# Turning xn and half of the probabilities on TensorE instead of through DRAM, in an attention block on one core

## What is computed

```python
def attn(x, Wq, Wk, Wv, Wo):
    q, k, v = x @ Wq, x @ Wk, x @ Wv
    scores = where(causal_mask, -max, einsum('bsd,btd->bst', q, k))
    attn = softmax(scores * dim_k ** (-0.5), axis=-1)
    return einsum('bst,btv->bsv', attn, v) @ Wo
...
x = x + layernorm(attn(layernorm(x), Wq, Wk, Wv, Wo))
x = x + layernorm(layernorm(x) @ W[idx] + b[idx])     # idx = argmax(log_softmax(logits) + gumbel(u))
```

## Time and profile before

| | before |
|---|---|
| median of 3 runs | 430.8 us (430.01 to 431.18) |
| the profiled execution | 428.95 us |
| its span from first to last instruction | 427.1 us |
| TensorE, VectorE, ScalarE, GpSimd busy | 384.1, 330.9, 259.3, 216.0 us |
| mean granted TensorE clock | 0.975 |
| moved by DMA | 67.75 MB, 54.5% of the queues' time on queue 1 |

### The profile page before, as it was taken

How to read it: one execution, slowest core, us unless ns; L and a number is a source line. 1 busy time by engine, 2 the same in 40 slices (tenths; PEclk the granted TensorE clock), 3 DMA queues, 4 the chain that set the end, 5 groups by cost and what they waited for, 6 DMA issues and landing times.

```text
span 427.1 us, 7846 instructions
## 1 busy us (share of the span) xinstructions
PE 384.1 (90%) x2652; PEld 359.5 (84%) x2652; DVE 330.9 (77%) x844; ACT 259.3 (61%) x642; POOL 216.0 (51%) x367
## 2 busy tenths in 40 slices
PE   7996967999869998999879998799979998999994
PEld 6775856999769996899769997699968997899994
DVE  4488755799847987789867998579868998667876
ACT  5866555576546665575655765567665757555642
POOL 5115264554645554645855446455656448535234
PEclk9998998999989998999999999899999999999998
DMA  6323884249843498328872498435982388331012
GB/s 196 119 55 122 240 221 115 69 171 254 229 130 103 193 240 238 115 69 271 232 190 81 163 262 243 126 114 199 272 219 82 120 241 237 105 107 51 25 51 74
DMA packets 45611, 67.75 MB, mean 159 GB/s; under 512 B 8196, under 2 KB 38276, under 8 KB 44676
## 3 DMA queue, kind: packets, MB, share of 16 engines
q1 hardware_dynamic: 45300, 66.99, 54.5%
q10 hardware_dynamic: 272, 0.26, 0.2%
HBM read 34.34 MB, written 32.90 MB: 157 GB/s over the span
## 4 chain that ended last, share of the span: by engine, by line
PE 45%; DMA 26%; issue 9%; DVE 7%; ACT 4%; POOL 3%; POOLq 3%; SPq 3%; DVEq 0%
PE bank L1003 25%; PE score L1003 17%; DMA p_kept<-p_turn 16%; DMA p_turn<-p_kept 9%; ACT pT_hi L704 3%; SPq L443 3%; PE bank L1157 2%; POOLq L517 2%; DVE p_turn L911 2%; POOL pT_lo L546 1%; DMA x_kept<-x_turn 1%; DVE neg_scores L901 1%; DVE g_lo L767 1%; ACT g_hi L582 1%; PE bank L1128 1%
## 5 line engine op out<-in xcount | busy, mean ns | idle before, releaser
L546 POOL TENSOR_TENSOR pT_lo<-p_turn,pT_hi 128x128 fp32r<-128x128 f32 (+7 forms) x60 | 82.2, 1393 | 22.2 <-ACT pT_hi L704 22.1
L1003 PE MATMUL bank<-v_hi,pT_lo 128*128 128x258 f32 x288 | 82.6, 287 | 7.0 <-DVEq L865 3.9
L1003 PE MATMUL bank<-v_lo,pT_hi 128*128 128x258 f32 x288 | 81.6, 283 | 0.0
L1003 PE MATMUL bank<-v_hi,pT_hi 128*128 128x258 f32 x288 | 81.2, 282 | 0.0
L1003 PE MATMUL score<-xT_hi,g_lo 128*128 128x384 f32 (+4 forms) x176 | 65.0, 369 | 15.0 <-DVE neg_max L901 14.9
L503 POOL TENSOR_TENSOR o_rstd<-o_ss,minus_half 128x1 f32<-128x1 f32 x64 | 37.9, 594 | 77.4 <-ACT squares_junk L738 77.4
L695 ACT ACTIVATE probs<-neg_scores,neg_max 128x128 f32<-128x128 f32 (+3 forms) x64 | 49.2, 776 | 42.0 <-DVE neg_max L901 41.9
L1003 PE MATMUL score<-xT_hi,g_hi 128*128 128x384 f32 (+4 forms) x176 | 63.2, 359 | 0.0
L1003 PE MATMUL score<-xT_lo,g_hi 128*128 128x384 f32 (+4 forms) x176 | 63.2, 359 | 0.0
L1003 PEld LDWEIGHTS bank<-v_hi,pT_lo 128*128 128x128 f32 x288 | 54.7, 190 | 8.5 <-issue 6.9
L1003 PEld LDWEIGHTS bank<-v_lo,pT_hi 128*128 128x128 f32 x288 | 54.9, 191 | 0.6
(11 more groups left out here) (115 smaller groups left out, 1031.3 us busy)
## 6 DMA issues: line engine op xcount, KB each, us to landing
x_sb<-in_L_attn_x_dram SPq DMA_DIRECT2D x32, 256.0 KB, 5.4
out_dram<-f_sb SPq DMA_DIRECT2D x31, 256.0 KB, 5.6
x_kept<-x_turn SPq DMA_DIRECT2D x7, 1024.0 KB, 4.3
x_turn<-x_kept SPq DMA_DIRECT2D x28, 256.0 KB, 7.1
p_kept<-p_turn SPq DMA_DIRECT2D x7, 960.0 KB, 9.8
p_turn<-p_kept SPq DMA_DIRECT2D x28, 240.0 KB, 4.2
p_kept<-p_turn SPq DMA_DIRECT2D x7, 704.0 KB, 3.1
p_turn<-p_kept SPq DMA_DIRECT2D x28, 176.0 KB, 4.4
```

The source lines that it names most:

```text
L546: nc.gpsimd.tensor_tensor(p_half(pT_lo, n), p_quads(n), p_half(pT_hi, n).bitcast(f32), ALU.subtract).then_inc(p_lo_ready, 1)
L1003: last = nc.tensor.matmul(dst, l, r, start=(i == 0), stop=(i == len(passes) - 1))
```

## The change

- xn is transposed by TensorE: 16 transposes of 128x128 a batch, in four jobs X0 to X3, into banks of the ring; ScalarE and VectorE split them from there. The blocks on VectorE (B), the write and the reads (W, R), `x_turn` and `x_kept` are gone.
- The probabilities of row tiles 0 to 3 are transposed by TensorE too (T0 to T3, ten transposes a batch, four jobs), in every batch, and split by ScalarE and VectorE. Tiles 4 to 7 still go through DRAM, in the last batch through TensorE as before.
- The ring has 32 jobs a batch instead of 24. `pT` has four places instead of three, counted over all batches, with a wait of ScalarE (`slot_read`) where the old content may still be read.
- All order strings are new. X2, X3 of the next batch are at the end of a step, their G2 and G3 in the next step.

```diff
-    PS = 3
+    PS = 4
-    PE_ORDER = """S0 S1 S2 S3 O6' O7' S4 Y1' V0 S5 Y2' F0' O0 S6 S7 O1 F1' V1 V2 Y3' F2' O2 V3 F3' O3 O4 O5 G0 G1 G2 Y0 G3"""
-    ACT_ORDER = """Y0' G3' E0 E1 E2 E3 O6' H0 O7' H1 P0 P1 Y1' E4 V0 H2 Y2' E5 O0 P2 F0' P3 H3 E6 O1 E7 V1 F1' V2 Y3' O2 P4
-        P5 V3 F2' O3 F3' X0 X1 O4 X2 X3 O5 G0 G1 P6 P7 G2"""
-    DVE_ORDER = """G2' M0 M1 G3' Q0 Q1 M2 Y0' M3 L0 L1 K0 K1 Q2 Q3 L2 K2 B0 R6' R7' M4 B1 Y1' Q4 V0 B2 M5 L3 F0' K3 Q5 Y2'
-        M6 N3' B3 Z0' M7 R0 R1 F1' Q6 V1 V2 Q7 Y3' F2' Z1' N0 R2 V3 F3' Z2' R3 N1 X0 X1 X2 X3 R4 R5 Z3'
-        G0 N2 G1"""
-    POOL_ORDER = """P7' L0 L1 C6' L2 C7' P0 P1 C0 L3 U0' P2 P3 N3' C1 U1' C2 P4 P5 U2' C3 N0 U3' N1 C4 C5 N2 P6"""
-    SP_ORDER = """P0 Q0 P1 A3' Q1 P2 W0 Z0' Q2 A0 R0 P3 Z1' Q3 A1 Z2' A2 Z3'"""
+    PE_ORDER = """S0 S1 F1' S2 Y2' G2' T0 S3 G3' O6' T1 T2 S4 O7' V0 S5 V1 T3 O0 S6 O1 Y3' F2' S7 Y0 O2 O3 V2 V3 F3' X0 X1
+        F0 O4 G0 Y1 G1 O5 X2 X3"""
+    ACT_ORDER = """X3' E0 P6' P7' E1 F1' Y2' G2' T0 E2 G3' H0 O6' T1 T2 E3 H1 E4 H2 O7' V0 V1 E5 T3 O0 O1 Y3' E6 F2' Y0 O2
+        E7 O3 V2 V3 P4 P5 X0 X1 H3 F3' F0 O4 G0 Y1 G1 O5 X2"""
+    DVE_ORDER = """M0 R5' X2' X3' M1 F1' M2 N2' L0 Y2' G2' T0 M3 L1 K0 G3' Z1' K1 L2 K2 T1 M4 T2 R6' Q4 R7' V0 N3' M5 V1 Q5
+        T3 M6 R0 L3 R1 Y3' F2' Q6 N0 M7 Y0 Z2' R2 Q7 R3 V2 K3 N1 V3 F3' X0 X1 F0 Z3' R4 G0 Y1 Z0 G1"""
+    POOL_ORDER = """P6' P7' N2' U1' L0 L1 L2 C6' C7' N3' C0 C1 U2' N0 C2 C3 L3 P4 P5 N1 U3' C4 U0 C5"""
+    SP_ORDER = """A2' Z1' A3' P2 A0 Q2 Z2' P3 A1 Q3 Z3' Z0"""
-    PE_LAST = """S0 V0 S1 S2 O6' S3 O7' Y1' S4 Y2' F0' O0 S5 Y3' S6 F1' V1 O1 V2 O2 V3 O3 F2' F3' T4 Y0 S7 Y1 T5 O4 T6 F0
-        O5 T7 O6 F1 Y2 O7 Y3 F2 F3 Y4 F4"""
+    PE_LAST = """S0 S1 S2 S3 T0 G2' T1 O6' G3' F1' Y2' T2 O7' V0 S4 F2' V1 O0 O1 V2 S5 T3 T4 O2 S6 S7 Y3' V3 Y0 O3 T5 F3'
+        Y1 T6 O4 O5 T7 F0 O6 Y2 O7 Y3 F1 F2 F3 Y4 F4"""
...
-                    elif kind == "W":
-
-                        sp.wait_ge(x_turned, b.count(NP, 0))
-                        sp.dma_start(x_kept.rearrange("p q r -> p (q r)"), x_turn[:, :]).then_inc(x_written, 16)
-                    elif kind == "R":
-                        sp.wait_ge(x_written, b.count(16, 0))
-                        fetch(x_turn[:, :], x_kept.rearrange("(i a) q r -> q a i r", i=QUADS), x_raw_loaded)
...
+            def slot_read(b, n, kind):
+
+                free, at = (b, n - PS) if n >= PS else (b.other(-1), n + NT - PS)
+                if not free.exists() or follows(in_act, (kind, n, b.known), ("O", at, free.known)):
+                    return
+                if kind == "T" and follows(in_pe, ("T", n, b.known), ("O", at, free.known)):
+                    return
+                used = Job(free, "O", at)
+                act.wait_ge(bank_full[used.bank], used.used + 1)
...
                     elif kind == "T":
+                        slot_read(b, n, "T")
                         for g, (u0, u1) in enumerate(t_groups(n)):
                             job = Job(b, "T", n, g)
-                            round_hi(job, pT_hi[:, n % PS, u0 * PART:u1 * PART], cols(job.bank, (u1 - u0) * PART))
+                            round_bank(job, pT_hi[:, (b.known * NT + n) % PS, u0 * PART:u1 * PART], cols(job.bank, (u1 - u0) * PART),
+                                       t_hi_ready)
...
-                        c, k = n // KC, n % KC
-                        if n == 0:
-                            act.wait_ge(x_raw_loaded, b.count(QUADS * 16, 0))
-                            act.wait_ge(scores_ready, b.count(NT, 0))
...
-                        nc.scalar.activation(split_block(xT_hi, c, k), raw_block(c, k),
-                                             ACT.Identity).then_inc(x_hi_ready, 1)
+                        x_hi(Job(b, "X", n), n, x_hi_ready)
...
-            def x_transposes(job, p):
-
-                pe.wait_ge(xn_ready, p + 1)
+            def x_transposes(b, job, p):
+
+                pe.wait_ge(xn_ready, b.count(NP, p + 1))
...
-                        if n % 2 == 0:
-                            pe.wait_ge(x_lo_ready[c], b.count(KC, 0))
-                        g_quarter(Job(b, "G", n), [], n)
+                        g_quarter(Job(b, "G", n), [] if n % 2 else [Job(b, "X", n), Job(b, "X", n + 1)], n)
+                    elif kind == "X":
+                        x_transposes(b, Job(b, "X", n), n)
```

More of the change, by code:

```diff
@@ L438, in _, with turned_pairs @@
                 load_x(Batch(0, 1), p)
+            def turned_pairs(b, n):
+                return sum(1 for (m, s) in turned if m == 2 * n + 1 and s <= b.known)
             def fetch(raw, kept, loaded):
@@ L448, in sequence @@
                     b = Batch(s, ahead)
-                    if not b.exists({"A": 2, "W": 1, "R": 1}.get(kind, 0)):
+                    if not b.exists(2 if kind == "A" else 0):
                         continue
@@ L688, in sequence @@
                             pass
-                        elif b.last and n - 2 in LAST_T:
-                            job = Job(b, "T", n - 2, len(t_groups(n - 2)) - 1)
+                        elif before_by_two(b, n) in turned:
+                            act.wait_ge(p_turned, turned[before_by_two(b, n)])
+                        elif before_by_two(b, n) in turned_by_pe and not follows(
+                                in_act, ("E", n, b.known), ("T", *before_by_two(b, n))):
+                            m, s = before_by_two(b, n)
+                            job = Job(Batch(s, 0), "T", m, len(t_groups(m)) - 1)
                             act.wait_ge(bank_full[job.bank], job.used + 1)
-                        elif b.known != 0 or n >= 2:
-                            act.wait_ge(p_turned, b.count(NT, n - 1))
                         here = slice(0, (n + 1) * PART)
@@ L697, in sequence @@
                     elif kind == "P":
[L699 to L704 removed]
+                        act.wait_ge(p_loaded[n // 2], QUADS * 16 * sum(
+                            1 for (m, s) in turned if m == n // 2 * 2 + 1 and s <= b.known))
+                        slot_read(b, n, "P")
+                        nc.scalar.activation(p_half(pT_hi, b, n), p_quads(n), ACT.Identity).then_inc(p_hi_ready, 1)
                     elif kind == "T":
+                        slot_read(b, n, "T")
                         for g, (u0, u1) in enumerate(t_groups(n)):
                             job = Job(b, "T", n, g)
[L708 removed]
+                            round_bank(job, pT_hi[:, (b.known * NT + n) % PS, u0 * PART:u1 * PART], cols(job.bank, (u1 - u0) * PART),
+                                       t_hi_ready)
                     elif kind == "V":
@@ L794, in x_means @@
                 last.then_inc(x_mv_ready, 1)
-            def x_blocks(b, p):
-                dve.wait_ge(xn_ready, b.count(NP, p + 1))
-                if b.known != 1 and p == 0 and not follows(in_dve, ("B", p, b.known), ("G", 3, b.known - 1)):
-                    for c in range(2):
-                        dve.wait_ge(x_lo_ready[c], b.count(KC, -KC))
-                turned = x_turn[:, :].rearrange("p (q k t s) -> p t k q s", q=QUADS, k=KC, t=NT)
-                for t in (2 * p, 2 * p + 1):
-                    last = nc.vector.transpose(turned[:, t], xn[:, t, :].rearrange("p (k q a) -> p k q a", k=KC, q=QUADS))
-                last.then_inc(x_turned, 1)
             def copy_transposed(n):
@@ L1140, in sequence @@
                         job = Job(b, "O", n)
-                        if b.last and n in LAST_T:
+                        if (n, b.known) in turned_by_pe:
                             take_bank(job, Job(b, "T", n, len(t_groups(n)) - 1), Job(b, "V", n // 2))
@@ L1148, in sequence @@
                         product(cols(job.bank, DE),
-                                [both(pT_hi, pT_lo, ALL, n % PS, slice(t * PART, (t + 1) * PART)) for t in range(n + 1)],
+                                [both(pT_hi, pT_lo, ALL, (b.known * NT + n) % PS, slice(t * PART, (t + 1) * PART)) for t in range(n + 1)],
                                 [both(v_hi, v_lo, ALL, t, ALL) for t in range(n + 1)]
```

126 lines of the change are left out of this document (49 added, 77 removed).

## The result

| | before | after |
|---|---|---|
| median of 4 runs each | 430.99 us (430.01 to 432.88) | 410.06 us (408.40 to 411.17) |
| the profiled execution | 428.95 us | 410.2 us |
| its span | 427.1 us | 408.2 us |

The ratio is 0.951, with a 95% interval of 0.946 to 0.955: 21 us, or 5%, faster. The forecast was 416 us with a range of 408 to 428. The sign and the mechanism were right, and the gain was under-estimated by 6 us: 410.06 stands at the low edge of the 410 to 421 that was called likeliest. (Tiles 0 to 3, which the title calls half of the probabilities, are half of the row tiles, but 10 of the 36 blocks of 128x128.)

A forecast was written before the change was run, and what follows sets the result against it. TensorE bounds the kernel, with pauses from DRAM turns. From a 427.1 us span: 5.6 less in the first step, 12.2 less in six steps, 3.3 more at the end, giving 412.6; profiled 414.4, median 416, range 408 to 428.

The forecast's parts named there:

- The bound: TensorE, busy 384.1 of 427.1 us; its 2.41 us pause before S2 comes from tiles 6 and 7 through DRAM.
- The steady step: Each of six middle steps, S2 to S2: 47.7 us against 49.74, 12.2 us less in all.
- Tight work: TensorE's work in a middle step packed without pauses: 44.2 us plus 26 transposes at 0.11, together 47.1.
- four tight places: F0, O4, O5 and S0, where TensorE needs something under 0.5 us after it is free: 0.6 us a step, bounds 0 and 2.4.
- The first step: Start to S2 of batch 1: 65.6 us instead of 71.20, 5.6 less, bounds 3 and 8.
- The new wait: First step: TensorE stands from about 30.5 to 34 us behind GpSimd's scale of the next x, priced at 3.5.
- The last stretch: From the last S2 to the end, 57.5 us before: 4.7 more, or 3.3 more with F1' counted here, bounds 2 and 6.
- Rival (A): VectorE's order makes the step: tight places slip, step 49.2 to 49.5 us, median 425 to 427; chance 0.18.
- (B): The clock falls with the transposes once a step, 1.5 us each: median 425; chance 0.06.
- (C): The ring of four banks turns too slowly for 32 jobs a step: median 432 or 447, slower than before; chance 0.09.
- The clock: Falls to 1.2 GHz behind pauses, 3 us long and costing 1.5 each, should go where the pauses go.
- A transfer: The 960 KB write should land in 4 to 6 us; ScalarE waiting over 4 us a step for P6's fetch would refute it.

The follow-up runs named there:

- The first experiment: Kernel before with only the rounding of probability tiles 6 and 7 moved behind the next batch's first exponential, all transfers kept: 414.77 us, ratio 0.961.

## Why the prediction was right, and where it was off

- **The bound.** It named TensorE as the bound and the turn of tiles 6 and 7, through ScalarE's queue, as the cause of the pause before S2. The first experiment confirms the second by itself; that TensorE bounds the kernel after is shown by the doubled transposes, which lengthen the step by all that they cost.
- **The steady step.** Forecast 47.7, measured 46.97. Tight work was forecast as 44.2 + 26 x 0.11 = 47.1. The doubled transposes give 0.112 each, so that 46.97 - 2.9 = 44.1 is the rest: right to 0.1. What was mis-sized is the term of 0.6 us for four tight places. It measured 0, the lower of its bounds. Together over six steps that is 6 x (0.6 + 0.13) = 4.4 us, the whole difference in the row of six steps. VectorE and GpSimd at F0, O4 and S0 in the kernel after:

```profile
241.16 0.66 DVE L758 TENSOR_TENSOR v_lo<-bank,v_hi 128x512 fp32r<-128x512 f32 x1
...
241.88 3.37 POOL L539 TENSOR_TENSOR pT_lo<-p_turn,pT_hi 128x640 fp32r<-128x640 f32 x2
...
242.24 0.36 PE L973 MATMUL bank<-wf_hi,yT_lo 128*128 128x256 f32 x1
...
243.74 0.28 PE L973 MATMUL bank<-v_hi,pT_lo 128*128 128x258 f32 x1
...
250.12 0.68 DVE L758 TENSOR_TENSOR g_lo<-bank,g_hi 128x512 fp32r<-128x512 f32 x1
```

  V3's low half ends at 241.82 and F0 starts at 242.24; P4's share of the 3.37 us (640 of 1408 columns) ends at about 243.4 and O4 starts at 243.74; O5's bank is free at 248.22 and O5 starts at 248.75; G1's low half ends at 250.80 and S0 starts at 251.76. The layout by hand was right about the place of each, with margins of 0.4, 0.3, 0.5 and 1.0 us. A place that is on time by 0.3 us cost nothing here.
- **The first step.** S2 of batch 1 at 65.6 was forecast and came at 66.42. The new wait is where it was put: TensorE stands 2.65 us before V0 at 33.12, behind H0 and the evictions of T1 and T2. M4, which the prediction has in that row, runs only after V0 has begun. The wait was priced at 3.5. Half of a fall of the clock was priced at 0.7, and a whole one came, 1.6. The small waits, priced at 1, were 0.9. So the work itself, put at 37.5 us, was about 38.4.
- **The last stretch.** 61.35 against 62.2: against before, TensorE's busy time in it is 3.7 us longer (forecast 3.5), and its idle time, priced at 1.2 us more, 0.2.
- **Around the span.** The median was put 1.85 us over the profiled execution, as before. Here the profiled one (410.2) is as good as the median (410.06). That adds the other 1.5 of the 5.9 us between 416 and 410.06; which of the executions is profiled is chance.
- **Rival (A)**: VectorE is busy for 37.90 of 47.00 us, as forecast (38 of 47.7), and TensorE never waits for it in a step. (Its price doesn't follow from its own terms: four places 0.6 to 0.8 late make a step of 49.5 to 50.3 and a median of 427 to 432, not 425 to 427.) **(B)** fell by the doubled transposes. **(C)**, the ring: eight rounds now fit in 46.97 us, 5.87 each, and no bank is waited for in a step. With three places of pT the mechanism of (C) does show, a bank held behind a wait on ScalarE, at 1.8 us a step. That is far from enough to be slower than before. (By the prediction's sum a round of 6.2 us would give 427 us, not yet slower; that begins at 6.3.)
- **The clock.** The falls in the steps are gone, as are the pauses there; one is left, 3.4 us behind the pause in the first step. Each was put at 3 us and 1.5 of cost, and measures 3.4 and 1.6. A pause made a fall possible, not certain: with three places of pT the same pause of 2.65 us had none behind it.
- **A transfer.** The write was expected in 4 to 6 us and took 4.3, and P6' never waited.
- **What the prediction didn't see**: it took the change as one thing and didn't ask which part earns its cost. One place in the orders earns 16 of the 21 us by itself, the ten transposes of tiles 0 to 3 cost 1.1 us a step that nothing gives back, and what xn's sixteen earn stays open.

The length of about 275 ns that the Trainium skill gives for a transpose inside a kernel, in a passage on bf16 (TensorE: Matmul & The Clock Gate, Part 4: PE-mode transpose), is what the trace has for one record, 272 to 274 ns for float32 in the groups of the kernel after. In a row they come one every 0.11 us, which is what the step pays. By that section the full clock doesn't engage for transposes; here, between other matmuls, it stayed at 1.00 with 52 of them in a step.

## What to carry to other kernels

On an engine that works in strict order, a step that waits for a transfer belongs behind whatever the bounding engine needs next; look for this before transfers are replaced by work. Once the bounding engine has no pause left, each operation put on it costs its full spacing, so work moved there to avoid a wait is worth trying back where it was when the wait is gone another way. Orders can be laid out by hand from the durations of a trace, but an order moved in one place moves the pause to the next tightest one, so each attempt needs its profile read.

## What the runs showed of the hardware that was not expected

- Transposes of 128x128 float32 on TensorE come one every 0.103 to 0.112 us, also 16 in a row, with records of 272 ns each, and leave the granted clock at 1.00.
- The write of 960 KB to DRAM lands in 9.7 to 9.8 us (medians) in each kernel that sends xn through DRAM as well (before, and three of the experiments), and in 4.3 to 4.4 us in those that don't (after, and tiles 0 to 3 through DRAM). The reads of 240 KB behind it take 4.1 to 4.6 us in either. In the trace of before, four reads of xn are in flight at each of these writes; the one issued at 251.56 lands 9.5 us later, and those reads at 255.7 to 258.8. Behind S2 it is issued at nearly the same place as in the kernel after (29.0 and 31.8 us). That the reads are the cause is likely, but no run separated them from the other transfers.
- A pause of 2.65 us on TensorE was followed by 3.4 us at a granted clock of 0.50 in the kernel after, and by none in the kernel with three places of pT, in the same place. Such a fall costs 1.6 us (43.54 against 41.95 us from S0 to the next S2). Pauses of 1.0 and 1.56 us in every step of two other kernels left the clock line at 9 in all its middle slices.
